# Attention over two tiles a round: maxima two tiles ahead, sums apart from the mixing, end-of-batch work in the next batch

## The reference, cut to what matters

```python
kv_r   = rope(kv_c)                                   # (32, 1500, 64)
q_r    = rope(norm(x) @ Wq ...) @ W_qr                # (32, 16 heads, 56, 64); only layer 0 ropes q
scores = einsum('bhsr,bhlr->bhsl', q_r, kv_r @ W_kr)  # (32, 16, 56, 1500)
attn   = softmax(scores, axis=-1)
ctx_c  = einsum('bhsl,bld->bhsd', attn, kv_r)
x      = x + (ctx_c @ w_kc_kv ...) @ Wo
```

## Time and profile before

| | |
|---|---|
| time, median of 3 runs | 3251.58 us (3242.52 to 3254.57) |
| the profiled execution | 3247.99 us, its span 3246.2 |
| TensorE busy | 2900.0 us, 89% of the span |
| VectorE, GpSimd, ScalarE busy | 60%, 51%, 37% |
| attention, layer 0 | from about 120 to 1440 us |
| attention, layer 1 | from about 1825 to 2870 us |
| one batch of layer 1, 1946.20 to 1973.16 | 26.96 us: TensorE 26.56, GpSimd 21.06, VectorE 16.74, ScalarE 12.34 busy |

### The profile page before, as it was taken

One profiled execution on the slowest core, in us unless ns is written; L12 is line 12 of the kernel. 1 busy time (PEld: TensorE's weight loads), 2 busy tenths in 40 slices (PEclk: granted clock), 3 DMA queues, 4 the chain that ended last, 5 costly groups with the idle time before them and its releaser, 6 DMA issues. The chain is left out here.

```text
span 3246.2 us, 42715 instructions
## 1 busy us (share of the span) xinstructions
PE 2900.0 (89%) x15992; PEld 1652.0 (51%) x15992; DVE 1960.3 (60%) x2318; ACT 1189.1 (37%) x1648; POOL 1663.3 (51%) x947
## 2 busy tenths in 40 slices
PE   7689899998998999996899799999989989978888
PEld 6544444444544454445788544444444444435565
DVE  3476667766766576745666556556456556645554
ACT  3124441444144414443333244434424434423222
POOL 0367775776576667762100077557737737730001
PEclk9689999999999999998999899999999999988889
DMA  8333331333133312312000333323413423210000
GB/s 281 88 88 82 85 95 36 80 79 99 33 81 81 103 38 72 79 34 83 1 1 1 73 75 81 73 51 81 94 31 82 94 49 78 58 52 1 6 6 12
DMA packets 102326, 212.32 MB, mean 65 GB/s; under 512 B 30690, under 2 KB 77778, under 8 KB 94572
## 3 DMA queue, kind: packets, MB, share of 16 engines
q1 hardware_dynamic: 102124, 209.59, 24.9%
HBM read 138.51 MB, written 46.00 MB: 57 GB/s over the span
## 5 line engine op out<-in xcount | busy, mean ns | idle before, releaser
L1044 POOL TENSOR_TENSOR sums<-sums,prob 125x896 f32<-125x896 f32 x544 | 1149.9, 2114 | 206.3 <-ACT prob L984 158.8
L1129 DVE TENSOR_REDUCE maxpart<-pair 112x2 f32<-112x1000 f32 x720 | 861.5, 1196 | 467.6 <-PE pair L862 467.4
L984 ACT ACTIVATE prob<-wide 125x896 f32<-125x896 f32 x768 | 704.6, 917 | 873.3 <-PE wide L888 866.6
L902 PE MATMUL single<-prob,kv 125*64 125x448 f32 x3072 | 755.1, 570 | 0.8
L883 PE MATMUL wide<-qhigh,kparts 64*125 64x448 f32 x3072 | 455.5, 374 | 8.3 <-DVE maxpart L1129 8.3
L862 PE MATMUL pair<-kparts,qhigh 64*112 64x500 f32 x1440 | 349.0, 481 | 72.3 <-DVE maxpart L1129 71.0
L862 PEld LDWEIGHTS pair<-kparts,qhigh 64*112 64x112 f32 x1440 | 126.1, 172 | 492.3 <-DVE maxpart L1129 423.6
L1044 POOL TENSOR_TENSOR sums<-prob 125x896 f32<-125x896 f32 x64 | 135.1, 2111 | 455.1 <-ACT prob L984 455.1
L883 PEld LDWEIGHTS wide<-qhigh,kparts 64*125 64x125 f32 x3072 | 279.0, 185 | 116.9 <-issue 78.5
L888 PE MATMUL wide<-shift,ones_row 64*125 64x448 f32 x1536 | 285.6, 366 | 10.9 <-DMA shift<-maxrow 10.9
L883 PE MATMUL wide<-qlow,kparts 64*125 64x448 f32 x1536 | 283.8, 364 | 0.0
(11 more groups left out here) (320 smaller groups left out, 3891.3 us busy)
## 6 DMA issues: line engine op xcount, KB each, us to landing
kparts<-keys_merged SPq DMA_DIRECT2D x64, 750.0 KB, 8.8
kparts<-kparts SPq DMA_DIRECT2D x96, 250.0 KB, 3.1
keys_merged<-kparts SPq DMA_DIRECT2D x32, 750.0 KB, 7.4
recip<-zrec_merged SPq DMA_DIRECT2D x124, 112.0 KB, 2.8
w_low_values<-w_merged SPq DMA_DIRECT2D x64, 192.0 KB, 2.4
raw<-in_ctx SPq DMA_DIRECT2D x32, 375.0 KB
values_merged<-kv SPq DMA_DIRECT2D x32, 375.0 KB
kv<-values_merged SPq DMA_DIRECT2D x32, 375.0 KB
```

The source lines that it names most:

```text
L902: mm = pe.matmul(mix_acc[64 * half:64 * half + DC, 0:HQ], kv[:, b % 3, t, :], prob[:, (b * LT + t) % NPROB, half * HQ:(half + 1) * HQ], st ...
L984: nc.scalar.activation(prob[:, n_ % NPROB, :].rearrange("p (a b) -> p a b", a=2), acc[0:LP, :, 0:HQ], ACT.Exp)\
L1044: nc.gpsimd.tensor_tensor(dst, first_in, prob[:, n_ % NPROB, :], ALU.add).then_inc(s["pool_sum"], 1)
L1129: V.tensor_reduce(maxpart[:, b % 2, t:NMAX:4, third], acc[0:TQ, :, 0:LB], AX.X, ALU.max).then_inc(*R.signal_drained(kind, *key))
```

## The change

- The loop goes by rounds of two tiles. TensorE's order in a round is: maxima, score, score, maxima, mix, mix, where the two mixes are those of the round before. Before, it was score, mix of the tile before, maxima, for every tile.
- The maxima are two tiles ahead instead of four, so 14 instead of 16 of them stand in the query phase, in another order and over the regions in turn.
- VectorE's additions have a step of their own, "sum", for the round's own tiles; GpSimd's stay in "mix". The total stands in a new step "total", in round 2 of the next batch, between the two maxima (in a query phase behind "context").
- "norm" moves from t = 1 to round 2, "spread" from the end of t = 8 to the start of round 6 (ahead of its first maxima), "share" stays at 10. The fetch of layer 1 stands at the start of round 2, as before at t = 2.
- Layer 0: rope at rounds 4 and 6, between the maxima (before t = 1 and 2); keyT at 4, 6 and 10 (3, 4, 5), its first third waits only for the first half of rope; ropecos at 10 and in the next round 0 (10 and 11); rotate at 8 (9); stash at round 2 of the batch behind (t = 11).
- The layer norm of the next group stands at rounds 0, 8 and 10 of the last batch (before, at t = 2 to 10 one by one).

```diff
-EARLY_MAX = 4
+        def leave():
+            for t in (LT - 2, LT - 1):
+                add("mix", old, t)
+            add("context", old)
+            add("total", old)
...
-            for t in range(LT):
-                ahead = (j + 1, t + EARLY_MAX) if t + EARLY_MAX < LT else (j + 2, t + EARLY_MAX - LT)
+            for t in range(0, LT, 2):
+                units = {u: (b + 1, u + 2) if u + 2 < LT else (b + 2, u + 2 - LT) for u in (t, t + 1)}
+                units = {u: unit for u, unit in units.items() if unit[0] < first + BG}
...
                 if layer == 1 and t == 2 and b + 2 < NB:
                     add("fetch", b + 2)
-                add("score", b, t, region=t % 2)
+                if t == 6 and j:
+                    add("spread", b - 1)
+                if t in units:
+                    maximum(*units[t])
+                if t == 2 and j:
+                    add("total", b - 1)
+                if layer == 0 and t in (4, 6) and b + 2 < NB:
+                    add("rope", b + 2, t // 2 - 2)
+                for u in (t, t + 1):
+                    add("score", b, u, region=u % 2)
+                if t + 1 in units:
+                    maximum(*units[t + 1])
                 if j + 1 < BG and t == 8:
                     add("maxneg", b + 1)
-                if last is not None:
-                    add("mix", *last)
-                    if last[1] == LT - 1:
-                        add("context", last[0])
-                last = (b, t)
-                if t == 1 and j:
+                if behind is not None:
+                    for u in range(2):
+                        add("mix", behind[0], behind[1] + u)
+                    if behind[1] == LT - 2:
+                        add("context", behind[0])
+                behind = (b, t)
+                for u in (t, t + 1):
+                    add("sum", b, u)
+                if t == 2 and j:
                     add("norm", b - 1, region=3)
-                if j + 1 < BG and t == 9:
+                if j + 1 < BG and t == 8:
                     add("maxT", b + 1, region=3)
...
-                if ahead[0] < BG:
-                    maximum(first + ahead[0], ahead[1])
-                if t == 8 and j:
-                    add("spread", b - 1)
+                if layer == 0 and t in (4, 6, 10) and b + 2 < NB:
+                    add("keyT", b + 2, (4, 6, 10).index(t), region=3)
+                if layer == 0 and t == 2 and b >= 1 and b + 1 < NB:
+                    add("stash", b + 1)
                 if t == 10 and j:
                     add("share", b - 1, 2)
+                if layer == 0:
+                    if t == 8 and b + 3 < NB:
+                        add("rotate", b + 3)
+                    if t == 10 and b + 3 < NB:
+                        add("ropecos", b + 3, 0)
+                    if t == 0 and b + 2 < NB:
+                        add("ropecos", b + 2, 1)
                 if g + 1 < G and j == BG - 2 and t == 4:
                     add("heads", g + 1)
                 if g + 1 < G and j == BG - 1:
-                    if t == 2:
+                    if t == 0:
                         add("mean", g + 1, region=3)
+                        for k in range(KT):
+                            add("square", g + 1, k)
-                    if t == 5:
+                    if t == 8:
                         add("var", g + 1, region=3)
+                        for part in range(2):
+                            add("rstd", g + 1, part)
-                    if t == 9:
+                    if t == 10:
                         add("xsplit", g + 1)
...
-                    pe.wait_ge(s["rope_done"], 2 * (b + 1))
+                    pe.wait_ge(s["rope_done"], 2 * b + min(third, 1) + 1)
...
-                elif kind == "mix":
+                elif kind == "sum":
...
-                elif kind == "context":
+                elif kind == "total":
```

More of the change, by code:

```diff
@@ L117, in attention_schedule @@
                 if n >= 6 and (n - 6) % 4 < 3:
[L118 removed]
+                    maximum(first, (n - 6) // 4 + 4 * ((n - 6) % 4))
                 if g and n == 5:
@@ L134, in attention_schedule @@
                     add("stash", 1)
-            for i in range(3):
-                maximum(first + 1, i, (0, 1, PAIR)[i])
+            maximum(first + 1, 0, 0)
             add("query", g, NPAIR - 1, region=2)
@@ L139, in attention_schedule @@
                 add("attn", g - 1, 0, region=1)
-            for c in range(3):
-                add("smax", first, 3, c, region=(0, PAIR, 0)[c])
+            for n in (3, 7, 11):
+                maximum(first, n, (0, PAIR, 0)[n // 4])
             if g:
@@ L145, in attention_schedule @@
             add("maxneg", first)
-            maximum(first + 1, 3)
+            maximum(first + 1, 1)
             add("maxT", first, region=3)
@@ L162, in attention_schedule @@
                 if p >= 4:
[L163 to L169, removed]
+                    maximum(first, (0, 4, 8, 1)[p - 4])
+            maximum(first, 5, 0)
+            maximum(first, 9)
+            if g:
+                add("share", old, 2)
+                add("attn", g - 1, 0, region=1)
+            maximum(first, 2, 0)
+            maximum(first, 6)
+            maximum(first, 10, 0)
             if g:
                 add("attn", g - 1, 1)
-            for c in range(3):
-                add("smax", first, 3, c, region=(PAIR, 0, 0)[c])
+            for n in (3, 7, 11):
+                maximum(first, n, (PAIR, 0, PAIR)[n // 4])
             if g:
@@ L176, in attention_schedule @@
             add("maxneg", first)
-            for i in range(2):
-                maximum(first + 1, i, (PAIR, 0)[i])
+            for n in range(2):
+                maximum(first + 1, n, (0, PAIR)[n])
             add("maxT", first, region=3)
@@ L181, in attention_schedule @@
                 add("attn", g - 1, 3)
-            for i in range(2, 4):
-                maximum(first + 1, i, (PAIR, 0)[i % 2])
-        last = None
+        behind = None
         for j in range(BG):
             b = first + j
-            for t in range(LT):
-                ahead = (j + 1, t + EARLY_MAX) if t + EARLY_MAX < LT else (j + 2, t + EARLY_MAX - LT)
+            for t in range(0, LT, 2):
+                units = {u: (b + 1, u + 2) if u + 2 < LT else (b + 2, u + 2 - LT) for u in (t, t + 1)}
+                units = {u: unit for u, unit in units.items() if unit[0] < first + BG}
@@ L189, in attention_schedule @@
                 if layer == 0 and b == 0 and t == 0:
                     add("rotate", 2)
[L191 to L194, removed]
+                    add("ropecos", 2, 0)
                 if layer == 1 and t == 2 and b + 2 < NB:
                     add("fetch", b + 2)
-                add("score", b, t, region=t % 2)
+                if t == 6 and j:
+                    add("spread", b - 1)
```

24 lines of the change are left out of this document (5 added, 19 removed).

## The result

The changed kernel takes 3288.5 us (median of 4 runs, 3278.8 to 3292.1) where the kernel before, on the same chip, takes 3250.1: a ratio of 1.013, with a 95% interval of 1.010 to 1.016. It is 38 us slower. The forecast was 3217 us, 31 faster. The profiled execution took 3292.1 us, 75 more than the sum gave from a profiled execution of 3248.0.

What follows compares the result with a forecast made beforehand. TensorE was taken to bound layer 1's loop, with VectorE's order deciding layer 0's stalls. From the profiled 3248.0 us, gains of 144 and losses of 113 gave 3217 us; forecast's own range 3190 to 3250, overall 3150 to 3285.

Steps and rivals of the forecast that it cites:

- The grouping: Loop's tile pairs: fewer passages between 64-row and 125-row products, 3.96 us a pair instead of 4.26, 115 us gained.
- rival C: Loop's tile pairs: second maxima break the row of scores, passages shorten by only 0.10 a pair, 3294 us; chance 0.10.
- SP's queue, layer 1: Packing of the sums lands with the fetch issued ahead; TensorE idles 3.0 us in 23 batches, 69 lost (0 to 104).
- Rival A: Layer 1's packing of the sums isn't held up by the fetch, 3151 us; chance 0.19.
- The granted clock: TensorE's clock falls after one in five of layer 1's 23 new waits, 1.7 us each: 8 lost (0 to 39).
- The norm of the next group: Group's end: norm chain at steps 8 and 10 delays the query products, 24 us lost (0 to 45).
- The end of the batch, layer 0: VectorE's keyT subtractions and other work make maxima 1.84, 0.87 and 0.67 us late; 12 us lost over four groups.
- Rival B: Layer 0, step 2: the total loses the port to GpSimd's sum, step 4's maxima 2.0 late, 3265 us; chance 0.17.
- The share: Layer 1, batch end: ctx_n behind step 10's last maxima lasts 1.2 us, following maxima 0.2 late; 4 us gained.
- the shift rows: SP's shift copies no longer stand behind the store of the reciprocals; TensorE waits less, 9 us gained.
- the maxima before the loop: Query phase: 14 instead of 16 maxima, alternating between two regions; 16 us gained over 8 groups (0 to 40).

## Why the prediction was wrong

Two terms of the sum failed, and both are of layer 1: the wait behind SP's queue was sized too small, and the granted clock behind that wait was put at next to nothing.

**The grouping** was right: 3.94 a round for a forecast of 3.96, and with it rival C falls. Its 115 us came as 82 in the changed kernel's order, since layer 0's longer rounds had hidden some of VectorE's lateness, and as 106 where they have little to hide.

**SP's queue, layer 1** was the right mechanism, sized too small: 4.1 us a batch, 94 in all, for 3.0 and 69. I let the packing land with the fetch, at 12.2 of step 2. Its last packet does end with the fetch's, at 12.3 us after the issue, but the reciprocal starts 0.8 behind that: 12.5 to 13.9 after the fetch's issue, and 14.5 to 14.9 in the group's seventh batch, in which SP also loads head weights. The upper bound, 104 us, held for the sum; five of the waits were longer than its 4.5. Rival A, to which I gave 0.19, was wrong: the packing never passed the fetch, and from another queue it gained 0.6 us.

**The granted clock** is the step that turned the sign together with it: 8 us forecast, 46 measured. I took the share, one wait in five, from waits of 2 us and used it for waits of 3; all 23 are 3.2 us or longer, and all of them were followed by half clock, at 3.4 or 6.8 us of it, where I had put 1.7 us lost on each at most. Even my bound of 39 was too low. Waits of 2.1 us lost it in 6 of 23. These two terms are 63 of the 75 us by which the sum failed, and without them (as with the reciprocal at step 8) the change is faster by 2.8%.

**The norm of the next group**: the chain from the root to the end of x_low took 9.8 us in layer 1 and 11.6 in layer 0, where I had put 8.6 and 1.1 more in layer 0; the share (1.15) stands in it too. TensorE stood 6.5 us (layer 1) for 5.1 and 7.75 (layer 0) for 6.2, 42.8 instead of 33.9 in six groups, with half clock behind it.

**The end of the batch, layer 0**: 1.84, 0.87 and 0.67 us late by the sum, 1.47, 0.52 and 0.44 measured; right in place and a little too dark. Rival B didn't happen: totals inside a group of layer 0 took 1.08 us at the median, and in the run with the total in step 0 the one that waited in layer 1 was GpSimd's sum. The mean of all totals rose to 1.32 us (1.08 in the earlier trace rows); a few, seven of 56, took 2.97 to 3.06.

**The share, the shift rows and the maxima before the loop** are small: the share takes 0.82 on average for 1.45, TensorE's wait for the shift falls from 10.9 to 4.1 us. From a group's last maxT copy to the second of the next group, a stretch that holds the query phase, it takes 100.9 us in layer 1 (102.2 before) and 147.7 in layer 0 (144.7). The forecast had +1.4 and +2.5, so layer 1 did better than forecast here although its wait for x_low was longer; no run takes that gain apart.

## What to carry to other kernels

A step that waits for a small transfer is only as early as the large transfer issued ahead of it: count from that one's issue to its end and 0.4 to 1.7 us more (medians of the runs here), on whatever queue, and put the waiting instruction behind work that is due before that. Here one instruction of 0.2 us, a step too early, cost some 135 us, more than the regrouping of all products had gained. When a wait of TensorE is forecast, price it with the clock behind it. Longer waits lost it more often: here those of 2.1 us on average in 6 of 23 cases, those of 3.2 in 18, and those of 4.1 in all, which made each microsecond of waiting one and a half. And when a step moves, its DMA moves as well, past every wait of the queue it stands in.

## What the runs showed of the hardware

- A packing of 1.8 KB a transfer, issued 5.2 us behind a fetch of 1.9 MB, is there 13.1 us after the fetch's issue (median of 23) from the same queue and 12.6 from ScalarE's. From either queue its first packet moves 8.1 us after the fetch's issue.
- A load of 125 rows keeps the DMA engines' share at 0.33 and 103 GB/s; the keys' 64 rows ran at 218 GB/s, and the values as 120 and 5 rows at a share of 0.71 and 139 GB/s, each packet of 3 KB taking 0.23 us instead of 0.12.
- After a wait of 3.2 us or more TensorE ran at its lower clock (1.2 in place of 2.4 GHz) for 3.4 or 6.8 us in 23 of 23 cases of the changed kernel, after waits of 3.1 to 5.3 us in 21 of 23 of the kernel with ScalarE's packing, after waits of 2.2 to 4.1 us in 18 of 23 of the kernel with 120 and 5 rows, and after waits of 1.4 to 3.7 us in 6 of 23.
- Where a total of VectorE and a sum of GpSimd came up 0.35 us apart, behind a reduction, VectorE's took its 1.08 us and GpSimd's 3.42 instead of 2.10, although its record starts first (24 of 24 cases of the run with the total in step 0).
